# Projections and attention of a transformer layer in one stage, with the first maxima placed between projections

## The reference

```python
q = (x @ wq.T).reshape(b, t, NUM_HEADS, 2, HEAD_DIM)
k = (x @ wk.T).reshape(b, t, NUM_HEADS, 2, HEAD_DIM)
v = (x @ wv.T).reshape(b, t, NUM_HEADS, 2 * HEAD_DIM)
attn = _attn(q1, k1, v) - lambda_full * _attn(q2, k2, v)     # softmax(q k / 4) v
attn = attn * rms * subln_w * (1 - LAMBDA_INIT)
return attn.reshape(b, t, 512) @ wo.T
```

## Time and profile before

| | us |
|---|---|
| median of 3 runs | 2691.18 (2689.74 to 2695.02) |
| the profiled execution | 2691.85 |
| its span, first to last instruction | 2690.1 |
| TensorE busy | 2448.0 (91%) |
| VectorE, ScalarE, POOL busy | 1707.7, 1206.9, 188.6 |
| projections of layer 0, last matmul | from 19.4, 152.5 |
| attention 0, first score | 210.4 |
| projections of layer 1, last copy of values | 1860.3 |
| attention 1, first score | 1903.6 |

### The profile page before, as it was taken

One profiled execution on the slowest core, in us unless ns is written; L12 is line 12 of the kernel. 1 busy time (PEld: TensorE's weight loads), 2 busy tenths in 40 slices (PEclk: granted clock), 3 DMA queues, 4 the chain that ended last, 5 costly groups with the idle time before them and its releaser, 6 DMA issues. The chain is left out here.

```text
span 2690.1 us, 41760 instructions
## 1 busy us (share of the span) xinstructions
PE 2448.0 (91%) x15600; PEld 1255.6 (47%) x15600; DVE 1707.7 (63%) x3976; ACT 1206.9 (45%) x1571; POOL 188.6 (7%) x341
## 2 busy tenths in 40 slices
PE   7958999999999999879999999877799999999886
PEld 5832222222222222357888888766233333333365
DVE  2146888888888888483444444432677777777586
ACT  2205666666666666552122222331355555555553
POOL 3000000000000000000000000000111111111103
PEclk9968999999999999899999999988799999999998
DMA  5373311113211100001000000015322212210001
GB/s 190 131 125 96 43 25 25 25 25 40 33 25 25 25 2 1 29 9 40 24 24 23 23 23 24 0 57 138 58 30 38 32 24 37 37 20 2 25 1 63
DMA packets 56645, 108.91 MB, mean 40 GB/s; under 512 B 11808, under 2 KB 22048, under 8 KB 56464
## 3 DMA queue, kind: packets, MB, share of 16 engines
q1 hardware_dynamic: 53936, 96.79, 18.3%
q0 software_dynamic: 2528, 9.70, 1.0%
HBM read 73.75 MB, written 31.46 MB: 39 GB/s over the span
## 5 line engine op out<-in xcount | busy, mean ns | idle before, releaser
L551 ACT ACTIVATE l_prob<-l_p_score 128x1024 f32<-128x1024 f32 (+2 forms) x896 | 827.9, 932 | 699.6 <-PE l_p_score L488 699.6
L583 DVE TENSOR_REDUCE l_maxima<-l_p_ring 128x1 f32<-128x512 f32 x1280 | 823.8, 685 | 232.2 <-PE l_p_ring L465 228.5
L508 PE MATMUL l_p_out<-l_prob,v_all 128*32 128x512 f32 (+3 forms) x3584 | 869.5, 561 | 10.1 <-ACT l_sums L542 6.1
L508 PE MATMUL l_p_out<-l_prob,l_ones 128*32 128x512 f32 (+3 forms) x3584 | 869.5, 561 | 0.0
L488 PEld LDWEIGHTS l_p_score<-xT_l_q,xT_l_k 50*128 50x128 f32 x1792 | 167.6, 184 | 645.7 <-ACT l_prob L551 487.1
L465 PE MATMUL l_p_ring<-xT_l_k,xT_l_q 48*128 48x512 f32 (+3 forms) x1792 | 363.7, 402 | 102.9 <-DVE l_maxima L580 54.0
L488 PE MATMUL l_p_score<-xT_l_q,xT_l_k 50*128 50x512 f32 (+3 forms) x1792 | 428.3, 475 | 13.5 <-DMA xT_l_q<-l_shift_rows 12.0
L580 DVE CUSTOM_DVE_ANT_0 l_masked_scores<-l_p_ring,mask 128x128 bf16<-128x128 f32 (+3 forms) x512 | 232.0, 488 | 117.6 <-PE l_p_ring L465 108.0
L508 PEld LDWEIGHTS l_p_out<-l_prob,v_all 128*32 128x32 f32 x3584 | 135.6, 108 | 275.1 <-issue 219.4
L465 PEld LDWEIGHTS l_p_ring<-xT_l_k,xT_l_q 48*128 48x128 f32 x1792 | 174.9, 192 | 148.2 <-DVE l_maxima L580 77.4
L1042 DVE SCALAR_TENSOR_TENSOR ffn_h<-ffn_p_u,ffn_group_scales,ffn_silu 128x512 f32<-128x512 f32 x64 | 48.0, 751 | 212.0 <-PE ffn_p_u L197 206.2
(11 more groups left out here) (141 smaller groups left out, 2761.4 us busy)
## 6 DMA issues: line engine op xcount, KB each, us to landing
xT_l_q<-q_parts SPq DMA_DIRECT2D x192, 128.0 KB, 5.5
q_parts<-l_part SPq DMA_DIRECT2D x64, 256.0 KB
xT_l_k<-k_parts SPq DMA_DIRECT2D x96, 128.0 KB, 7.6
k_parts<-l_part SPq DMA_DIRECT2D x40, 256.0 KB
xT_l_k<-k_parts SPq DMA_DIRECT2D x96, 64.0 KB, 4.9
x<-in_x_T SPq DMA_DIRECT2D x4, 1024.0 KB, 11.2
xT_l_q<-l_shift_rows SPq DMA_DIRECT2D x256, 4.0 KB
x<-in_L_attn_x POOLq DMA_DIRECT2D x1, 4096.0 KB, 16.0
```

Source lines behind the costliest of these rows:

```text
L508: summing = pe.matmul(p_out[r0:r0 + VD, off:CH], lhs, prob[step % PRING][:, sub, off:CH], start=first, stop=final)
L551: act.activation(prob[step % PRING][:, :, off:CH], p_score[:, step % 2, :, off:CH], ACT.Exp, scale=HD ** -0.5).then_inc(exped, 1)
L583: dve.tensor_reduce(to, scores, AX.X, ALU.max).then_inc(freed, 1)
```

## The change

`qkv_phase` is dropped, and its work moves into `attention_phase`, in one block without the barrier. The item list now begins with projections:

```diff
+QK_BANKS = 3
+V_BANKS = 2
+PART_BUFFERS = 3
+LOAD_SLOTS = 4
-        self.items = self.order()
+        self.items = self.projections() + self.heads()
+    def projections(self):
+        MT = self.q_tiles + self.k_tiles
+        work = []
+        for c in range(NCH):
+            work += [("unit", c * MT + m) for m in range(MT)] + [("values", c * QPC + t) for t in range(QPC)]
+        out, at, shift_at = [], 0, None
+        start = QC * (MT + QPC) + LOAD_SLOTS
+        for i, item in enumerate(work):
+            out.append(item)
+            if shift_at == i:
+                out.append(("shift", 0))
+            while i >= start and at * (len(work) - start) < self.first_pairs * (i + 1 - start):
+                out.append(("pair", *divmod(at, len(self.pairs))))
+                at += 1
+                if at == len(self.pairs):
+                    shift_at = i + 1
+        return out
-L0 = Layer("l0", D, D, False, 0.35)
-L1 = Layer("l1", D // 4, D // 4, True, 0.45)
+L0 = Layer("l0", D, D, False, 0.6, 26)
+L1 = Layer("l1", D // 4, D // 4, True, 0.6, 19)
```

A q buffer is now half the k-tiles of xT of one batch, so buffers 0 and 1 are free when batch 0 is projected, 2 and 3 when batch 1 is. SP's list:

```diff
+                else:
+                    sp.wait_ge(v_done, NT // B * (i // 2 + 1))
...
+            for what, *at in L.items:
+                if what == "unit":
+                    store(*at)
+                    if L.shift_store == at[0]:
+                        shift_row(0)
+                elif what == "values" and at[0] == NT // B - 1:
+                    wait_stored(QC * MT)
+                    load(0)
+                    sp.wait_ge(ready, 3)
+                    load_ones(0)
+                    load(1)
+                    load_ones(1)
+                elif what == "score":
+                    break
+            if L.shift_store is None:
+                shift_row(0)
+            wait_stored(L.units)
+            for i in range(2, PAIR_BUFFERS):
+                load(i)
+                load_ones(i)
+            for n in range(1, HEADS):
```

```diff
                 if n == 0 and s == 0:
+                    pe.wait_ge(part_lo, L.units)
+                    pe.wait_ge(v_kept, NT)
                     pe.wait_ge(ones_in, 16 * PAIR_BUFFERS * 2 * KH)
```

More of the change, by code:

```diff
@@ L90, in __init__ @@
         self.qc_last = [max(s for s, x in enumerate(self.steps) if x[0] == qc) for qc in range(QC)]
-        self.lead = lead
-        self.items = self.order()
+        self.lead, self.first_pairs = lead, first_pairs
+        self.items = self.projections() + self.heads()
+        later = [x[1] for x in self.items[self.items.index(("shift", 0)):] if x[0] == "unit"]
+        self.shift_store = later[1] if len(later) > 1 else None
         self.filled_at, self.bank_at = {}, {}
@@ L109, in order @@
         stream = [(n, u) for n in range(HEADS) for u in range(len(self.pairs))]
[L110 to L113, removed]
+        out, at = [], self.first_pairs
+        spent = sum(cost[u] for _, u in stream[len(self.pairs):at])
         ready = []
-        out.append(("shift", 0))
         goal = self.lead * sum(cost)
@@ new lines, in attention_phase @@
+        ones_rows = attn_area.taken_by(f"{L.name}_ones_rows", [2, T], F32R, NT * D - T)
+        ones = sb("ones", [P, VD], F32)
+        maxima = sb("maxima", [P, 2, 2 * KT, 2], F32)
+        shift = sb("shift", [P, 2 * KT], F32)
+        shift_rows = [sb(f"shift_rows{i}", [2 * KT, P], F32R) for i in range(2)]
+        if L.causal:
+            masked_scores = [sb(f"masked_scores{i}", [P, CH], BF16) for i in range(2)]
+            mask, mask_made = sb("mask", [P, CH], F32), sem("mask_made")
+        recip = sb("recip", [P, QPC, 2], F32)
@@ L248, in _ @@
[L248 to L349, removed]
-        sb = lambda n, s, d: ctx.enter_context(nc.sbuf_tensor(f"{L.name}_{n}", s, d))
-        ps = lambda n, s, d: ctx.enter_context(nc.psum_tensor(f"{L.name}_{n}", s, d))
-        sem = lambda n: ctx.enter_context(nc.semaphore(f"{L.name}_{n}"))
-        q = [rooms[0].taken_by(f"{L.name}_q{i}", [P, 2, T], F32R, i * 2 * T) for i in range(PAIR_BUFFERS)]
-        k = [rooms[1].taken_by(f"{L.name}_k{i}", [P, KH, T], F32R, i * 2 * T) for i in range(PAIR_BUFFERS)]
-        prob = [sb(f"prob{i}", [P, 2, CH], F32) for i in range(PRING)]
-        ones = sb("ones", [P, VD], F32)
-        ones_rows = sb("ones_rows", [2, T], F32R)
-        maxima = sb("maxima", [P, 2 * KT, 2], F32)
-        shift = sb("shift", [P, 2 * KT], F32)
-        shift_rows = [sb(f"shift_rows{i}", [2 * KT, P], F32R) for i in range(2)]
-        masked_scores = [sb(f"masked_scores{i}", [P, CH], BF16) for i in range(2)]
-        sums = sb("sums", [P, CH], F32)
-        recip = sb("recip", [P, QPC, 2], F32)
-        half = sb("half", [P, 2, QPC, VD], F32)
-        p_score = ps("p_score", [P, 2, 2, CH], F32)
-        p_ring = ps("p_ring", [P, RING, CH], F32)
-        p_out = ps("p_out", [P, CH], F32)
@@ L369, in attention_phase @@
+        stored = [sem(f"stored{r}") for r in range(PART_BUFFERS)]
         q_in = [sem(f"q_in{i}") for i in range(PAIR_BUFFERS)]
@@ new lines, in store @@
+            def store(u):
+                c, m = divmod(u, MT)
+                dst, mm, dims = (q_parts_d, m, D) if m < L.q_tiles else (k_parts_d, m - L.q_tiles, L.k_dims)
+                first = (c // QC) * (dims // HD) + mm * (P // HD)
+                sp.wait_ge(part_lo, u + 1)
+                for i in range(PARTS):
+                    sp.dma_start(dst[first:first + P // HD, i * HD:(i + 1) * HD, (c % QC) * CH:(c % QC + 1) * CH],
+                                 part[u % PART_BUFFERS][i][:, :].bitcast(F32)).then_inc(stored[u % PART_BUFFERS], 16)
@@ L433, in _ @@
             pool.memset(ones_rows[:, :].bitcast(F32), 1.0).then_inc(ready, 1)
+            if L.causal:
+                pool.memset(mask[:, :], 0.0).then_inc(mask_made, 1)
+                pool.wait_ge(mask_made, 1)
+                pool.affine_select(out=mask[:, CH - P:CH], in_=mask[:, CH - P:CH], compare_op=ALU.is_ge, fill=MASKED,
+                                   base=0, pattern=[[-1, P]], channel_multiplier=1).then_inc(mask_made, 1)
+            if first_load:
+                for c in range(1, NCH):
+                    pool.wait_ge(x_in[c], 16)
+                    for i in range(KD):
+                        at = (slice(None), i, slice(c * CH, (c + 1) * CH))
+                        pool.tensor_copy(xT.hi[at], x_stage[at]).then_inc(pool_hi, 1)
+                        pool.wait_ge(pool_hi, (c - 1) * KD + i + 1)
+                        pool.tensor_tensor(xT.lo[at], x_stage[at], xT.hi[at], ALU.subtract).then_inc(pool_lo, 1)
             for n in range(HEADS):
```

165 lines of the change are left out of this document (116 added, 49 removed).

## The result

The changed kernel takes 2726.01 us in the median of four runs (2723.92 to 2731.63), the kernel before 2693.10 in four runs beside it. The ratio is 1.0122, with an interval of 1.0094 to 1.0149: slower by 33 us, where the forecast had +16 and the range ended at 2726. The profiled execution took 2727.58 us with a span of 2725.9, 35.8 more than before.

What follows compares the result with a forecast made beforehand. TensorE was taken as busy 91%, idle mainly at two seams set by the q and k loads. Layer 0's seam +13.9, layer 1's +10.3 and steady order -8 gave +16.2 on 2691.85: 2708 us, range 2680 to 2726.

Steps and rivals of the forecast that it cites:

- The stall at pair (0,1): Projections, second maxima pair: TensorE stands while stores queue behind two early loads, 20.7 us in layer 0, 15 in layer 1.
- V7's copy: Copy of values tile 7, after which SP issues the early loads; tile done at 87.5 and 1822.2 us.
- U19's copy: Layer 0, ScalarE's copy of projection tile 19: waits until tile 16's store, queued behind both loads, lands at 118.
- The last hole: Between projections and first score: two late loads and their ones rows take 28 us in layer 0, 21.2 in layer 1.
- stores that slip past: Rival, both seams: DMA engines interleave stores with the early loads, layer 0 7.1 better, layer 1 4.3: 2697 us; chance 0.13.
- the term for the clock, 2.7 us per seam: Projections behind each stall: lowered granted clock costs 2.7 us per layer, from a stretch granted 0.85 over 20 us.
- The price of a pair, 0.5: Maxima pair among projections: 0.5 us of TensorE each, between 0.33 in a steady step and 0.80 at half clock.
- The waits of the doubles: Two maxima pairs in a row among projections, the second waiting for VectorE's reduction: 7.2 us in layer 0, 5.3 in layer 1.
- In layer 0 the order gains nothing: Layer 0's attention steps: TensorE is already full there, so the new steady order brings no gain.
- The steady order of layer 1, -8: Layer 1's attention steps: lead of 0.6 for 0.45 shortens the doubles' waits, -8 us over 31 heads, ends -16 and +9.
- the stall does not come: Rival, both seams: no wait before pair (0,1), so the change works as drawn and is faster, 2670 us; chance 0.15.
- ones 3 is SP's last: First score, layer 0: waits for all four buffers' ones rows, the last behind loads 2 and 3; score at 225.6, 15.2 later.

Runs made afterwards that it cites:

- x1: Changed kernel with all eight values tiles first in the second batch, then the q and k tiles: 2711.04 us, 1.0066 of the kernel before.
- y3: Changed kernel with only load 0 between the projections, load 1 and its ones rows going with loads 2 and 3: 2712.99 us, one run.
- x3: Changed kernel with one maxima pair per projection tile, never two, leftover pairs behind the last tile: 2697.69 us, 1.0015 of the kernel before.
- y2: Kernel before with only the lead of 0.6 in both layers and the maxima tile in two halves: 2682.36 us, ratio 0.9957.
- x2: Changed kernel with each buffer's ones rows counted with its own load, first score not waiting for all four: 2678.29 us, 0.9949 of the kernel before.
- x4: Changed kernel with x1, x2 and x3 together: 2641.81 us, ratio 0.9808 to the kernel before.
- x5: x4 with the first pair six (layer 1: eight) tiles behind the load instead of four: 2622.87 us, 0.9739 of the kernel before.

## Why the prediction was right and wrong

**Right: the direction and its waits.** The stall at pair (0,1) was forecast until 123.1 and 1851.2; pair (0,1) came at 123.26, and in layer 1 28.0 us behind V7's copy where 29.0 had been worked out. The idle times were 20.39 and 14.12 for 20.7 and 15; U19's copy came at 118.76 for 118. The last hole was taken as 28 and 21.2 and is 27.14 and 20.49 of idle time. The rivals fall with their marks: stores that slip past would have had that copy before 110, and x1 and y3 show the stall answering to what stands in the queue. The whole time of 2726.01 lies at the edge of the range and not near 2708, so the sum is what failed.

**Wrong: the term for the clock, 2.7 us per seam.** This is the step that failed. It was taken from one stretch before, 210 to 230 with 0.85 granted, and put in once for each stall. Laid out by tiles, the projections behind the stall go so:

- Layer 0, from pair (0,1) to the last pair at 202.41, 79.2 us for 74.5: 19 tiles with one pair at 3.38 make 64.2; the first of them at half clock, 2.6 more; the five doubles 3.7, 2.1, 3.7, 1.3 and 1.3, 12.1; the shift 0.3. The clock is 5.8 of it, 2.6 behind the stall and 3.2 behind two doubles.
- Layer 1, from pair (0,1) to the last pair at 1921.34, 55.3 us for 41.8. At full clock five tiles of 3.33 and eight values tiles of 1.9 (the last at full clock in x3) make 31.9, the waits of the four doubles in the trace 4.7, a wait of 0.5 before one other pair, the second pairs of the doubles 2.1, the shift 0.3: 39.5. The 15.8 that remain are put down to the clock, at 0.50 for 30 of these 55 us and, mostly behind two doubles, for 9 more.
- Behind the first score: layer 0 is granted 0.71 over the first 20 us of attention for 0.85 before, 2.8 us more. In layer 1 the clock is at 0.50 for 19 us behind the first score; in the kernel before it was for 12, of which 3 came after a return to full. The first two heads take 48.0 us for 45.0, 3.0 more. The prediction had nothing here, and this hides half of the gain of the steady order.

Together 3.1 + 13.1 + 2.8 + 3.0 = 22.0 us that the sum did not have, more than the 19.6 by which the span missed it. In layer 1 the numbers are a remainder, not a measurement of the clock alone; x3 supports them: without the doubles the same tiles, from pair (0,1) at 1850.05 to the last values copy at 1887.52, take 37.5 us.

**The price of a pair, 0.5.** It is 0.66: 3.38 a tile for 2.72. The end at half clock, 0.80, was nearer than the step at full clock that I leaned to. That is 2.9 us in layer 0 and 1.7 in layer 1. The waits of the doubles were well sized: 3 x 1.58 + 2 x 0.79 = 6.3 for 7.2, and 4.7 for 5.3.

**Too high by some us elsewhere.** "In layer 0 the order gains nothing" failed in the good direction: from 260 to 1100 us the weight loads of pairs waited 7.6 us for reductions before and not at all after, and a head takes 28.34 us for 28.46, 3.5 over the layer. The 2.7 us of the stretches before V7, between the layers and at the end were not traced to a cause.

**The steady order of layer 1, -8.** Right in its sign and 2 us too large: behind the first two heads the steps take 580.9 us for 586.7, 5.8 less (y2: 6.1), and TensorE is busy 92.74 of 100. That y2 as a whole shows -9.2 for the forecast -8 is in part luck, since 3.1 of it is what the first two heads gained at a clock that was back sooner.

**The chances.** The faster rival was "the stall does not come". That was the wrong hinge: x1 takes the stall away in layer 0, halves it in layer 1 and is still slower, by 0.66%. Without the doubles the loss is gone, within the noise (x3), and without the first score's wait for all four buffers it is a gain (x2). The prediction used this wait in its sum ("ones 3 is SP's last") and never questioned it.

## What to carry to other kernels

When a barrier goes, look at the waits that were cheap only because of it. Here one counter gathered four buffers, which cost little while all four loads stood together, and 48 us once two of them came late. A transfer put ahead of stores in one queue holds these stores for all of its data (here 13.5 us from issue to the copy behind two loads, 9.5 behind one), so what needs a buffer back must not stand right behind it. And price a short repeated wait by the spacing of the tiles around it, not by the wait alone: the clock that it costs can be as much again.

## What the runs showed of the hardware

- After a wait of 1.58 us between projection tiles, TensorE ran the next tile at half clock in two cases of three in layer 0 of the kernel after (7.05 us from copy to copy for 3.37), and after waits of 0.79 in neither of two. In x2 and y3 it was the same two of three, in x1 three of four.
- How long the half clock lasts differed with the work that followed. Behind a stall of 20.39 us the full-size projections of layer 0 were slow for one tile; behind 14.12 us the smaller tiles of layer 1 stayed at 0.50 for 20 us with TensorE busy 19.13 of them. The length of the gap does not set this: over such small tiles the clock stayed at 0.50 for 14 us behind a wait of 7.50 (x4, TensorE busy all the time) and for 18 us behind one of 6.24 (y3), and in both was full again only with the q and k tiles that came next. In x5 these tiles ran ahead of the first pair and of any wait, and the clock was full (1.00 from 1785 to 1800).
- The first scores of layer 1 ran at 0.50 for 19 us behind a hole of 20.49, for 8 us behind one of 28.92 (x1), and for 22 us behind none (x4). No run here shows what sets this time.
- A pair of products on 48 rows costs 0.66 us between products of the full array and 0.33 between attention products. Its own duration is 0.50 in the one and 0.40 in the other; the rest of the difference was not looked into.
